# Attention: the queries of four tiles projected in one pass, and a new order of the work around them

## The chip, the cores and the metric

The kernel runs on one core of a Trainium2 chip. The metric is the device time of one execution in microseconds (us). The engines named below are TensorE (PE in the rows, with PEld for its weight loads), VectorE (DVE), ScalarE (ACT), GpSimd (POOL) and SyncE (SP). Each runs its own list of instructions strictly in program order and waits on semaphores for the others.

## The reference, cut to what matters

A token mixing product feeds a gated linear attention, and a two-layer local attention with feed-forward layers follows. The change is in the linear attention alone. The inputs are 4 batches of 1024 tokens of 256 features; there are 16 heads of 64.

```python
q, k, v = (split_heads(x @ W) for W in (Wq, Wk, Wv))       # x: layernorm of h
g = sigmoid(split_heads(x @ Wg + bg))
q = elu(q) + 1.0
k = elu(k) + 1.0
kv = einsum('bhnd,bhne->bhde', k, v)
k_sum = k.sum(axis=-2)
z = 1.0 / clip(einsum('bhnd,bhd->bhn', q, k_sum), 1e-06)
out = einsum('bhnd,bhde->bhne', q * SCALE, kv) * z[..., None] * g
h = h + merge_heads(out) @ Wo
h = h + ffn(layernorm(h))                                  # two layers, unchanged
```

## The kernel before

**Tiles and stages.** A tile is 128 tokens, so a batch has TB = 8 tiles. The 16 heads form PAIRS = 8 pairs of two. Each batch runs in two parts. The first loops over the 8 tiles: `keys` projects a tile, ScalarE takes the exponential, VectorE makes the feature elu + 1, and `g_products` adds the tile's share of x-transposed times k. Then `kv_products` makes kv. The second part runs over STAGES = 4 stages `u` of two tiles each. A stage projects its queries (`queries`), its gates (`gates`), multiplies queries by kv (`outputs`, in three groups of 5, 6 and 5 pairs over the two tiles, listed in `CUTS`), and lets VectorE divide and gate the result (`gated`). The following stage transposes that result (`out_transposes`), splits it in a high and a low part (`ot_hi` on ScalarE, `ot_lo` on VectorE), multiplies by Wo (`out_products`) and adds to the residual stream (`residual`). From stage 1 on, two tiles of the next batch are prepared beside it: `normalise`, `xt` (their transposes), `x_high` and `low`. In the last batch there is no next batch; VectorE and ScalarE prepare tables and weights of the local attention there (`scale_table`, the copies into `local_h` and the subtractions into `local_l`, and two `x_copy`).

**Precision by three products.** `matmul3` makes each product of three matmuls, from high and low parts of both operands (lines L117 to L119).

**Features of the queries.** `queries(b, u, f)` projects two pairs of heads for the two tiles of stage `u` into one PSUM bank: 12 matmuls of 256 columns. ScalarE's `exp_` (L512) reads the bank, and `feature` on VectorE does a min on the exponential (L648) and then adds the positive part out of the bank (L652) into the tile `qt` (attn_qT). Two banks, 0 and 1, take turns. A projection may start only when the feature made from the same bank's former filling is done:

```python
pe.wait_ge(*s.attn_feat.room(n, 2))
```

**Banks 6 and 7** take turns in the same way for all transposes and for the products with Wo: `room(k, 2)` on `attn_t_done` means that filling k waits until VectorE is done with filling k - 2. The order of the fillings of a stage is two halves of `out_transposes(…, 0)`, `out_products(…, 0)`, two halves of `out_transposes(…, 1)`, `out_products(…, 1)`, and then the two `xt` of the next batch, which VectorE frees in `low`.

**Outputs** use banks 4 and 5 without a second copy: `outputs` of a group waits until `gated` has read the group before (L700), and `gated` multiplies by the gate in L704. Stage `u` starts its first `outputs` only when all its features are there.

**What sets the order.** Nothing but the order in which the code of each engine is written; there is no scheduler. The functions below issue it.

## Time and profile before

| | |
|---|---|
| runs shown | 1814.84, 1820.49 and 1815.06 us, median 1815.06 us |
| profiled execution | 1819.65 us; span from first to last instruction 1817.9 us |
| mean granted clock of TensorE | 0.996 |
| busy time in the span | TensorE 1771.5 us, VectorE 1395.9 us, ScalarE 1003.8 us, GpSimd 528.0 us |
| attention's stages | the first matmul of the queries starts at 112.2 us, the last of the `outputs` at 605.5 us |

Times of rows are in microseconds from the start of the span. The busy time of TensorE counts overlapping matmuls once, and the start of the next matmul says more of its pace than the length of one: a matmul's own length holds the time through the array as well.

### The profile page before, as it was taken

The page shows a single profiled execution, that of the slowest core. Times are in us where ns is not written, and L with a number is a line of the kernel's source. Part 1 is how long each engine was busy: PE and PEld are TensorE (multiplying, and loading weights), DVE is VectorE, ACT ScalarE, POOL GpSimd, SP SyncE. Part 2 cuts the span into 40 slices and gives each one's busy share as a digit, 9 for nine tenths or more (in the row PEclk, how much of TensorE's full clock was granted, in tenths as well). Part 3 has the DMA queues.
Part 4 walks back from the last instruction along what each step waited for, and adds up shares of the span by engine and source line. Part 5 has one row for each costly group of instructions (what it writes and reads, how often), then busy time and mean ns, then how long its engine had stood idle before and what let it go on. Part 6 is the DMA issues. An engine that isn't in the chain of part 4 may idle for free. (4 is left out here: it accounts for less than half of the span.)

```text
span 1817.9 us, 52839 instructions
## 1 busy us (share of the span) xinstructions
PE 1771.5 (97%) x19744; PEld 1554.0 (85%) x19744; DVE 1395.9 (77%) x4325; ACT 1003.8 (55%) x2481; POOL 528.0 (29%) x382
## 2 busy tenths in 40 slices
PE   8999999999999989999999999999999999989998
PEld 7879889889888778888888888888888888888887
DVE  5877877877867788888888687767888888877774
ACT  4443443443434478888887444337777777743333
POOL 0000000000000256666666000016666666611111
PEclk9999999999999999999999999999999999999999
DMA  9200000000020111111111200002111111110011
GB/s 330 83 1 2 2 1 2 1 1 2 1 72 2 40 41 29 26 29 26 29 27 35 100 12 12 1 1 70 28 27 29 27 26 29 32 35 12 6 66 33
DMA packets 64830, 60.44 MB, mean 33 GB/s; under 512 B 16415, under 2 KB 59211, under 8 KB 64718
## 3 DMA queue, kind: packets, MB, share of 16 engines
q1 hardware_dynamic: 64718, 58.88, 10.9%
q8 instruction: 78, 1.28, 0.3%
q14 instruction: 34, 0.28, 0.1%
HBM read 33.95 MB, written 8.39 MB: 23 GB/s over the span
## 5 line engine op out<-in xcount | busy, mean ns | idle before, releaser
L1317 ACT ACTIVATE l_probs<-l_probs,l_negmax 128x192 f32<-128x192 f32 x512 | 225.8, 442 | 86.6 <-DVE l_negmax L1424 86.6
L1142 POOL TENSOR_TENSOR l_t<-l_t,l_rnorm 128x512 f32<-128x512 f32 x128 | 136.1, 1083 | 245.5 <-DVE l_rnorm L1096 245.5
L1264 POOL TENSOR_TENSOR l_probs<-l_probs,l_rowinv 128x768 f32<-128x768 f32 x128 | 185.1, 1466 | 20.1 <-DVE l_rowinv L1453 20.1
L117 PE MATMUL ps<-local_w_hi,l_xT 128*128 128x512 f32 x384 | 158.0, 412 | 1.6 <-PEq L1719 1.1
L1272 POOL TENSOR_TENSOR l_t<-l_t,l_t 128x1024 f32<-128x1024 f32 x62 | 146.9, 2370 | 30.0 <-DVE l_t L1110 18.4
L118 PE MATMUL ps<-local_w_lo,l_xT 128*128 128x512 f32 x384 | 151.6, 395 | 0.0
L119 PE MATMUL ps<-local_w_hi,l_xT 128*128 128x512 f32 x384 | 151.3, 394 | 0.0
L117 PE MATMUL ps<-m_hnT_hi,ffn_w_hi 128*128 128x512 f32 (+1 forms) x352 | 141.0, 400 | 0.0
L512 ACT ACTIVATE attn_exp<-ps 128x512 f32<-128x512 f32 x128 | 76.4, 599 | 116.1 <-PE ps L119 116.1
L119 PE MATMUL ps<-m_hnT_hi,ffn_w_lo 128*128 128x512 f32 (+1 forms) x352 | 138.5, 394 | 0.0
L118 PE MATMUL ps<-m_hnT_lo,ffn_w_hi 128*128 128x512 f32 (+1 forms) x352 | 138.4, 393 | 0.0
L488 POOL MEMSET l_xT<- 128x520 f32 x1 | 0.5, 532 | 463.9 <-PE ps L897 463.9
L1588 PE MATMUL ps<-l_probsT,l_v 128*64 128x64 f32 x2048 | 126.0, 225 | 1.7 <-DVE x L1392 1.0
L1588 PE MATMUL ps<-l_probsT,l_edge 128*64 128x64 f32 x2048 | 123.0, 222 | 0.0
L1105 DVE TENSOR_TENSOR l_t<-ps,rope_c 128x1024 f32<-128x1024 f32 x64 | 78.4, 1225 | 51.6 <-PE ps L1568 46.1
L1834 ACT ACTIVATE m_gelu<-ps,ffn_b 128x512 f32<-128x512 f32 x80 | 55.0, 687 | 110.4 <-PE ps L119 110.4
L1323 ACT ACTIVATE l_probsT<-ps 128x512 f32<-128x512 f32 x192 | 101.1, 598 | 18.9 <-PE ps L1575 14.2
L117 PE MATMUL ps<-attn_w_hi,attn_xT_hi 128*128 128x512 f32 x256 | 107.3, 419 | 3.5 <-issue 1.9
L1588 PEld LDWEIGHTS ps<-l_probsT,l_v 128*64 128x64 f32 x2048 | 104.2, 138 | 6.4 <-ACT l_probsT L1323 2.1
L525 ACT ACTIVATE attn_tanh<-ps 128x512 f32<-128x512 f32 x64 | 38.3, 598 | 121.1 <-PE ps L119 121.1
L1588 PEld LDWEIGHTS ps<-l_probsT,l_edge 128*64 128x64 f32 x2048 | 104.5, 138 | 0.0
L118 PE MATMUL ps<-attn_w_lo,attn_xT_hi 128*128 128x512 f32 x256 | 101.1, 395 | 0.0
(273 smaller groups left out, 5709.1 us busy)
## 6 DMA issues: line engine op xcount, KB each, us to landing
l_edge<-l_v SPq DMA_DIRECT2D x252, 64.0 KB, 2.0
tok_x<-x SPq DMA_DIRECT2D x16, 512.0 KB, 8.0
shifted<-x SPq DMA_DIRECT2D x64, 64.0 KB, 1.5
m_shifted<-shifted SPq DMA_DIRECT2D x16, 256.0 KB, 2.8
out<-x SPq DMA_DIRECT2D x8, 512.0 KB, 3.2
ffn_w_raw<-ffn_w SPq DMA_DIRECT2D x6, 640.0 KB
local_w_raw<-ffn_wqkv SPq DMA_DIRECT2D x4, 768.0 KB, 5.2
tok_base<-attn_base SPq DMA_DIRECT2D x4, 512.0 KB, 9.0
```

Of the source, the lines that this page charges most:

```text
L117: nc.tensor.matmul(out, wh, mh, start=start, stop=False, skip_group_check=True)
L118: nc.tensor.matmul(out, wh, ml, start=False, stop=False, skip_group_check=True)
L119: return nc.tensor.matmul(out, wl, mh, start=False, stop=stop, skip_group_check=True)
L512: nc.scalar.activation(ex[:, at % 2], ps[:, at % 2], ACT.Exp).then_inc(s.attn_exp.sem, 1)
L1105: nc.vector.tensor_tensor(t1[:].rearrange("p a (h d) -> p a h d", d=DH), q, cw, ALU.mult)
L1142: return nc.gpsimd.tensor_tensor(v, v, rn[:, a * LH:(a + 1) * LH].unsqueeze(2).to_broadcast([P, LH, DH]), ALU.mult)
L1264: nc.gpsimd.tensor_tensor(v, v, rinv[:, heads].unsqueeze(2).to_broadcast([P, LH // 2, REACH]), ALU.mult).then_inc(s.normal.sem, 1)
L1272: nc.gpsimd.tensor_tensor(t1[:], t1[:], t2[:], ALU.add).then_inc(s.summed.sem, 1)
L1317: last = nc.scalar.activation(v, v, ACT.Exp, bias=nb[:, h:h + 1], scale=-1.0, accum_out=rsum[:, h:h + 1])
L1323: nc.scalar.activation(pt[:, 4 * k:4 * k + 4].rearrange("p b q -> p (b q)"), ps[:, PT[k]], ACT.Copy).then_inc(s.p_done.sem, 1)
L1588: last = nc.tensor.matmul(ps[e * DH:(e + 1) * DH, OT, pair * P + tokens.start:pair * P + tokens.stop], keys, pt[:, 3 * pair + block, token ...
L1834: nc.scalar.activation(gl[:, c % 2], ps[:, bank + 1], ACT.Gelu, bias=K.b1[:, layer, HC + c:HC + c + 1]).then_inc(s.gelu.sem, 1)
```

## The change

Stages 0 and 1 now share their queries, and so do stages 2 and 3. `queries(b, u, *pairs)` projects one pair of heads for four tiles, so that one filling of a bank is 6 matmuls of 512 columns. There are 8 fillings for stages 0 and 1 (pairs 0 to 7) and 8 for stages 2 and 3, as many as before, of the same 512 columns. `query_features` does the min as before, and then writes the two halves of the bank apart: tiles of the even stage to `qt`, tiles of the odd stage to a new tile (`attn_qT_odd`), which lies where the parts of the keys lay. So the first of them in a batch waits for the last `g_products`. `outputs` of stages 0 and 1 wait for all 8 features.

The order around them is new on three engines:

- TensorE: the fillings of pairs 2 to 7 stand in one run behind `kv_products`. Stage 0 ends with the first `out_transposes` of stage 1 straight behind its last `outputs`, and one half of a gate later the product with Wo follows; the same at the end of stage 2. `out_transposes(…, 1)` stands straight behind `out_products(…, 0)` in stages 1 and 3. Pairs 0 and 1 of stage 2 are projected at the end of stage 1, and pairs 2 to 7 between the transposes and products of stage 2.
- VectorE: `take_kv` stands ahead of `variance` and of the subtraction for Wo's low part; three features stand behind those. At the end of stage 1 two features, with a gating between them, stand ahead of the next batch's `low`. In stage 2 the residual stands ahead of the second gating.
- ScalarE: the exponentials follow the queries' new order.

```diff
@@ -430,6 +430,8 @@
+    (qt_key,), _ = mem.place(mem.wb + 2 * INNER * 4, mem.wa, ("attn_qT_odd", [P, PAIRS, 2 * P], F32))
+    (qt_last,), _ = mem.place(mem.wa + KC * INNER * 4, mem.norm, ("attn_qT_odd_last", [P, PAIRS, 2 * P], F32))
...
+    def queries_of(b, u):
+
+        return qt if u % 2 == 0 else qt_last if b == B - 1 else qt_key
...
-            def query_feature(b, u, f):
-                feature(AB * b + 16 + 4 * u + f, f, qt[:, 2 * f:2 * f + 2, :])
+            def query_features(b, u, *pairs):
+
+                for m in pairs:
+                    n = AB * b + 16 + 4 * u + m
+                    dve.wait_ge(*s.attn_exp.after(n + 1))
+                    chain(nc.vector.tensor_scalar(ex[:, m % 2], ex[:, m % 2], 1.0, None, ALU.min))
+                    if u == 0 and m == 0:
+                        dve.wait_ge(*s.attn_g_mm.after(TB * b + TB))
+                    for w in range(2):
+                        cols = slice(2 * w * P, 2 * (w + 1) * P)
+                        done = nc.vector.scalar_tensor_tensor(queries_of(b, u + w)[:, m], ps[:, m % 2, cols], 0.0,
+                                                              ex[:, m % 2, cols], ALU.max, ALU.add)
+                    done.then_inc(s.attn_feat.sem, 1)
...
-                query_feature(b, 0, 0)
-                query_feature(b, 0, 1)
+                query_features(b, 0, 0, 1)
+                take_kv(b)
+                query_features(b, 0, 2, 3, 4)
                 early.variance(nc, chain) if last else norm.variance(nc, chain)
...
-                take_kv(b)
-                query_feature(b, 0, 2)
-                query_feature(b, 0, 3)
+                query_features(b, 0, 5, 6, 7)
...
+                    if u == 1:
+                        query_features(b, 2, 0)
+                        gated(b, 1, 2)
+                        query_features(b, 2, 1)
                     if not last:
                         for w in range(2):
                             low(b + 1, 2 * u - 2 + w)
...
-            def queries(b, u, f):
-                n = AB * b + 16 + 4 * u + f
-                pe.wait_ge(*s.attn_feat.room(n, 2))
-                for i in range(2):
-                    m = 2 * f + i
+            def queries(b, u, *pairs):
+
+                for m in pairs:
+                    n = AB * b + 16 + 4 * u + m
+                    pe.wait_ge(*s.attn_feat.room(n, 2))
                     for c in range(KC):
...
+                        tokens = slice(2 * u * P, (2 * u + 4) * P)
+                        last = matmul3(nc, ps[:, m % 2], wh[:, Q, c, m * P:(m + 1) * P], wl[:, Q, c, m * P:(m + 1) * P],
+                                       xth[:, c, tokens], xtl[:, c, tokens], c == 0, c == KC - 1)
+                    last.then_inc(s.attn_a_full.sem, 1)
...
-                queries(b, 0, 2)
-                queries(b, 0, 3)
+                queries(b, 0, 2, 3, 4, 5, 6, 7)
...
+                for u in range(STAGES):
+                    if u == 1 or u == 3:
+                        gates(b, 2 * u, (0,))
+                        if first and u == 1:
+                            pe.wait_ge(*s.attn_wo_lo.after(1))
+                        out_products(b, last, u, 0)
+                        out_transposes(b, last, u, 1)
+                        gates(b, 2 * u, (1,))
+                    if u == 2:
+                        queries(b, 2, 2)
+                        out_transposes(b, last, 2, 0)
+                        queries(b, 2, 3, 4)
+                        out_products(b, last, 2, 0)
+                        queries(b, 2, 5)
+                        out_transposes(b, last, 2, 1)
+                        queries(b, 2, 6, 7)
+                        gates(b, 4)
...
+                    if u == 1 or u == 3:
+                        out_products(b, last, u, 1)
+                    if u == 1:
+                        queries(b, 2, 0)
...
+                    if not ending:
+                        outputs(b, u, 2)
+                    if u == 0 or u == 2:
+                        out_transposes(b, last, u + 1, 0)
+                    if u == 1:
+                        queries(b, 2, 1)
+                    if not last and u % 2:
+                        for w in range(2):
+                            xt(b + 1, 2 * u - 2 + w)
```

How the order moves on VectorE is shown at two places. The first is batch 0, behind the features of the first fillings. L157 to L164 are `variance`, attn_wo_lo is the subtraction for Wo's low part, attn_kv the copy of kv, L648 and L652 (now L748 and L753) the two steps of a feature. Before:

```order
L163 TENSOR_SCALAR attn_rstd<-attn_rstd 128x8
L164 SCALAR_TENSOR_TENSOR attn_dev<-attn_tmp,attn_rstd 128x8
L764 TENSOR_TENSOR attn_wo_lo<-attn_wo_raw,attn_wo_hi 128x2048
L711 COPY attn_kv<-ps 128x260 x2
L648 TENSOR_SCALAR attn_exp<-attn_exp 128x512
L652 SCALAR_TENSOR_TENSOR attn_qT<-ps,attn_exp 128x512
```

Now, from the feature of pair 4 on:

```order
L748 TENSOR_SCALAR attn_exp<-attn_exp 128x512
L753 SCALAR_TENSOR_TENSOR attn_qT<-ps,attn_exp 128x256
L753 SCALAR_TENSOR_TENSOR attn_qT_odd<-ps,attn_exp 128x256
L157 TENSOR_REDUCE attn_rstd<-attn_stats 128x8
L158 TENSOR_SCALAR attn_mean<-attn_rstd 128x8
L159 TENSOR_TENSOR attn_dev<-attn_stats,attn_mean 128x16
L160 TENSOR_TENSOR attn_dev<-attn_dev 128x16
L161 TENSOR_REDUCE attn_tmp<-attn_dev 128x8
L162 TENSOR_REDUCE attn_rstd<-attn_stats 128x8
L163 TENSOR_SCALAR attn_rstd<-attn_rstd 128x8
L164 SCALAR_TENSOR_TENSOR attn_dev<-attn_tmp,attn_rstd 128x8
L792 TENSOR_TENSOR attn_wo_lo<-attn_wo_raw,attn_wo_hi 128x2048
```

The copy of kv moved ahead of both, and the statistics and the subtraction now stand between the features of pairs 4 and 5, in the middle of TensorE's run of projections.

The second place is the end of stage 1 on VectorE. L640 and L642 (now L656 and L658) are `low`, which frees banks 6 and 7; L678 (now L694) is `residual`; L714 to L720 are the four steps of a gating. Before:

```order
L678 TENSOR_TENSOR h<-ps,h 128x256
L640 TENSOR_TENSOR attn_xn_lo<-attn_xn,attn_xn_hi 128x256
L642 TENSOR_TENSOR attn_xT_lo<-ps,attn_xT_hi 128x2x128
L640 TENSOR_TENSOR attn_xn_lo<-attn_xn,attn_xn_hi 128x256
L642 TENSOR_TENSOR attn_xT_lo<-ps,attn_xT_hi 128x2x128
L648 TENSOR_SCALAR attn_exp<-attn_exp 128x512
```

Now:

```order
L694 TENSOR_TENSOR h<-ps,h 128x256
L748 TENSOR_SCALAR attn_exp<-attn_exp 128x512
L753 SCALAR_TENSOR_TENSOR attn_qT<-ps,attn_exp 128x256
L753 SCALAR_TENSOR_TENSOR attn_qT_odd<-ps,attn_exp 128x256
L714 TENSOR_SCALAR attn_den<-ps 128x10
L715 RECIPROCAL attn_z<-attn_den 128x10
L716 TENSOR_TENSOR attn_out<-ps,attn_z 128x640
L720 SCALAR_TENSOR_TENSOR attn_out<-attn_tanh,attn_out 128x640
L748 TENSOR_SCALAR attn_exp<-attn_exp 128x512
L753 SCALAR_TENSOR_TENSOR attn_qT<-ps,attn_exp 128x256
L753 SCALAR_TENSOR_TENSOR attn_qT_odd<-ps,attn_exp 128x256
L656 TENSOR_TENSOR attn_xn_lo<-attn_xn,attn_xn_hi 128x256
```

Ten instructions of features and gating moved in between the residual and `low`.

## Rows read from the trace of the kernel before

**Rows 1.** The page, busy time by engine (share of the span, instructions).

```profile
PE 1771.5 (97%) x19744; PEld 1554.0 (85%) x19744; DVE 1395.9 (77%) x4325; ACT 1003.8 (55%) x2481; POOL 528.0 (29%) x382
```

**Rows 2.** Timeline, TensorE, batch 1: start, length, line, tiles, [idle before <- releaser].

```profile
233.10 0.39 PE L117 MATMUL ps<-attn_k_hi,attn_xn_hi 128*128 128x512 f32 x1
...
251.23 0.39 PE L119 MATMUL ps<-attn_k_hi,attn_xn_lo 128*128 128x512 f32 x1
...
259.40 0.28 PE L118 MATMUL ps<-attn_xT_lo,attn_w_hi 128*128 128x256 f32 x1
...
262.03 0.28 PE L119 MATMUL ps<-attn_xT_hi,attn_w_lo 128*128 128x256 f32 x1
```

**Rows 3.** Timeline, ScalarE and VectorE, one filling's exponential and feature, batch 1.

```profile
262.35 0.60 ACT L512 ACTIVATE attn_exp<-ps 128x512 f32<-128x512 f32 x1 [0.84 <-PE ps L119]
...
296.52 0.60 ACT L512 ACTIVATE attn_exp<-ps 128x512 f32<-128x512 f32 x1 [0.84 <-PE ps L119]
...
297.15 0.43 DVE L648 TENSOR_SCALAR attn_exp<-attn_exp 128x512 f32<-128x512 f32 x1 [0.28 <-ACT attn_exp L512]
297.61 0.69 DVE L652 SCALAR_TENSOR_TENSOR attn_qT<-ps,attn_exp 128x512 f32<-128x512 f32 x1
```

**Rows 4.** Timeline, VectorE's feature in stage 1 and TensorE's projection behind it.

```profile
275.66 0.69 DVE L652 SCALAR_TENSOR_TENSOR attn_qT<-ps,attn_exp 128x512 f32<-128x512 f32 x1
...
276.41 0.39 PE L117 MATMUL ps<-attn_xT_hi,attn_w_hi 128*128 128x256 f32 x1 [0.32 <-DVE attn_qT L652]
```

**Rows 5.** Timeline, VectorE, batch 1: `low` of one tile and the residual.

```profile
292.31 0.42 DVE L678 TENSOR_TENSOR h<-ps,h 128x256 f32<-128x256 f32 x1 [2.01 <-PE ps L119]
293.84 0.43 DVE L640 TENSOR_TENSOR attn_xn_lo<-attn_xn,attn_xn_hi 128x256 fp32r<-128x256 f32 x1 [1.10 <-ACT attn_xT_hi L505]
294.18 0.42 DVE L642 TENSOR_TENSOR attn_xT_lo<-ps,attn_xT_hi 128x256 fp32r<-128x256 f32 x1
```

**Rows 6.** Timeline, VectorE, `variance` (first step, and what follows its eighth), batch 1.

```profile
259.50 0.17 DVE L157 TENSOR_REDUCE attn_rstd<-attn_stats 128x8 f32<-128x16 f32 x1
...
261.15 0.77 DVE L711 COPY attn_kv<-ps 128x260 f32<-128x260 f32 x2
```

**Rows 7.** Timeline, batch 0: the subtraction on VectorE and TensorE's wait for kv.

```profile
122.26 2.29 DVE L764 TENSOR_TENSOR attn_wo_lo<-attn_wo_raw,attn_wo_hi 128x2048 fp32r<-128x2048 f32 x1
...
125.33 0.47 PE L117 MATMUL ps<-attn_w_hi,attn_xT_hi 128*128 128x512 f32 x1 [1.90 <-issue]
```

**Rows 8.** Windows, batch 0: length, busy time by engine, granted clock (0.50), DMA.

```profile
126.40:129.50 3.10, 3.10 (x9) 2.31 (x7) 2.49 (x12) 0.60 (x1) 0.00 (x0) 0.50 0.00 0
```

**Rows 9.** Timeline, TensorE, batch 1: groups of `outputs`, and four transposes of `xt`.

```profile
264.99 0.81 PE L924 MATMUL ps<-attn_kv,attn_qT 64*64 64x65 f32 x40
265.73 0.50 PE L117 MATMUL ps<-attn_w_hi,attn_xT_hi 128*128 128x512 f32 x1
...
292.95 0.66 PE L855 MATMUL ps<-ident,attn_xn 128*128 128x128 f32 x4
293.36 0.36 PE L117 MATMUL ps<-attn_xT_hi,attn_w_hi 128*128 128x256 f32 x1
```

**Rows 10.** Timeline, VectorE, stage 1 of batch 1: a gating's first, third and fourth steps.

```profile
285.44 0.17 DVE L698 TENSOR_SCALAR attn_den<-ps 128x10 f32<-128x10 f32 x1 [0.56 <-PE ps L924]
...
285.89 0.82 DVE L700 TENSOR_TENSOR attn_out<-ps,attn_z 128x640 f32<-128x640 f32 x1
286.75 0.82 DVE L704 SCALAR_TENSOR_TENSOR attn_out<-attn_tanh,attn_out 128x640 f32<-128x640 f32 x1
```

**Rows 11.** Timeline, high parts on ScalarE and low parts on VectorE, two halves each.

```profile
297.01 1.08 ACT L534 ACTIVATE attn_oT_hi<-ps 128x512 fp32r<-128x512 f32 x2
...
298.21 1.28 DVE L671 TENSOR_TENSOR attn_oT_lo<-ps,attn_oT_hi 128x512 fp32r<-128x512 f32 x2
```

**Rows 12.** Timeline, last batch, end of stage 2 on ScalarE: weights, then `x_copy`.

```profile
583.16 2.00 ACT L597 ACTIVATE local_w_hi<-local_w_raw 128x1024 fp32r<-128x1024 f32 x2
585.05 1.08 ACT L546 ACTIVATE l_x<-h,l_shift,l_rstd 128x256 f32<-128x256 f32 x2
```

More of the change, by code:

```diff
@@ L806, in batch @@
                         x_lo(0)
+                    if u == 2:
+                        residual(b, last, u, 1)
                     gated(b, u, 1)
@@ L811, in batch @@
                         turn(0)
-                    residual(b, last, u, 1)
+                    if u != 2:
+                        residual(b, last, u, 1)
+                    if u == 1:
+                        query_features(b, 2, 0)
+                        gated(b, 1, 2)
+                        query_features(b, 2, 1)
                     if not last:
@@ L924, in outputs @@
                             last = nc.tensor.matmul(ps[tokens, 4 + e, at:at + OC],
-                                                    qt[r, m, which * P + half * DH:which * P + (half + 1) * DH], kv[r, m, :],
+                                                    queries_of(b, u)[r, m, which * P + half * DH:which * P + (half + 1) * DH], kv[r, m, :],
                                                     start=True, stop=True)
@@ L999, in batch @@
                 gates(b, 0)
-                outputs(b, 0, 0)
-                gates(b, 1, (0,))
-                outputs(b, 0, 1)
-                gates(b, 1, (1,))
-                queries(b, 1, 0)
-                outputs(b, 0, 2)
-                for u in range(1, STAGES):
-                    if u > 1:
-                        queries(b, u, 0)
-                    queries(b, u, 1)
-                    out_transposes(b, last, u, 0)
-                    queries(b, u, 2)
-                    queries(b, u, 3)
-                    if first and u == 1:
-                        pe.wait_ge(*s.attn_wo_lo.after(1))
-                    out_products(b, last, u, 0)
-                    gates(b, 2 * u, (0,))
-                    out_transposes(b, last, u, 1)
-                    gates(b, 2 * u, (1,))
-                    if last and u == STAGES - 1:
+                for u in range(STAGES):
[6 more added lines that the diff above has]
+                        gates(b, 2 * u, (1,))
+                    if u == 2:
+                        queries(b, 2, 2)
[6 more added lines that the diff above has]
+                        gates(b, 4)
+                    ending = last and u == STAGES - 1
+                    if ending:
                         x_t(0)
@@ L1024, in batch @@
                     gates(b, 2 * u + 1, (0,))
+                    if u == 2:
+                        out_products(b, last, 2, 1)
                     outputs(b, u, 1)
                     gates(b, 2 * u + 1, (1,))
-                    if last and u == STAGES - 1:
+                    if ending:
                         outputs(b, u, 2)
```

50 lines of the change are left out of this document (26 added, 24 removed).

## Prediction

> **What bounds the kernel now.** I read the page first: TensorE is busy 1771.5 of 1817.9 us, the next engine 1395.9 us [rows 1]. TensorE is full, so an edit pays only if it shortens TensorE's list or one of its waits, and costs as soon as it adds one. Then I read the timeline of batch 1, engine by engine, and looked at the starts of matmuls. In a full stretch 512 columns start every (251.23 - 233.10) / 80 = 0.2266 us, and 256 columns every (262.03 - 259.40) / 22 = 0.1195 us [rows 2]. Waits within the stages are few. The fourth projection of stage 1 in each batch waits for a feature: 0.32 us idle [rows 4] and 0.16 us more if one counts from its slot, since a matmul of 256 columns lasts 0.28 us and its slot is 0.12 [rows 2], so 0.48 us. In batch 0 TensorE waits 1.90 + 0.16 = 2.06 us for the copy of kv, held up behind Wo's subtraction [rows 7]. Half of the clock (0.50 of 2.4 GHz, so 1.2 GHz) was granted for about 3 us behind that wait [rows 8].
>
> **Fewer, wider matmuls.** A filling of a bank was 12 x 0.1195 = 1.434 us and is 6 x 0.2266 = 1.360 us [rows 2]. There are 16 fillings a batch before and after, 64 in all, with the same columns, so the sum is 64 x 0.0744 = **-4.8 us**. The Trainium skill says so from its side too: "TensorE: Matmul & The Clock Gate", section "Back-to-back issue gap", gives columns / 2.4 + 2.5 ns, by which the pieces are 109.2 and 215.8 ns and the whole gain would be 384 x 2.6 ns = 1.0 us. The rows disagree with it at both widths, and the sum goes by the rows.
>
> **Waits taken away.** The wait in stage 1, 0.48 us and 0.10 us for the slower first step behind a wait, goes with its projection: 4 x 0.58 = **-2.3 us** [rows 4]. In batch 0 the copy of kv comes earlier and 2.06 + 0.10 us go: **-2.2 us** [rows 7]. Whether the low clock goes too depends on the next waits; I leave it as it is (its 3.1 us at half speed cost 1.6 us [rows 8]).
>
> **The run of projections.** This decides. What must pass between the end of a filling and the next use of the same bank? The exponential starts 0.20 us behind the last matmul's slot (262.35 against 262.03 + 0.12) [rows 2, 3]. VectorE starts 0.63 us later, and its second step 0.46 us after that (296.52, 297.15, 297.61) [rows 3]. The second step was one instruction of 0.69 us. Now it is two of 256 columns. Rows of that width start 0.34 us apart and last 0.42 us [rows 5], which gives 0.76 us; it can't be under the 0.69 us of one of 512, nor above 2 x 0.69 = 1.38 us. I take 0.76, since those rows read PSUM at the same width. Then TensorE starts 0.06 us later (275.66 + 0.69, 276.41) [rows 4]. Sum: 0.20 + 0.63 + 0.46 + 0.76 + 0.06 = 2.11 us. The other bank's filling covers 1.36 us. So a run waits 0.75 us at every second filling. Before, no more than two projections stood in a row ahead of other work, so this never showed. Now six stand in a row (pairs 2 to 7), and pairs 4 and 6 wait: 2 x (0.75 + 0.10) = 1.7 us a batch.
>
> Pair 7 waits for more. Between the features of pairs 4 and 5 VectorE now does `variance`, 261.15 - 259.50 = 1.65 us [rows 6]. Stepped through for batch 1 from kv_products' end at 259.0: pair 4 projected 262.6 to 264.1, its feature done on VectorE at 266.0, `variance` to 267.65, feature 5 done and seen at 269.0; TensorE is through with pair 6 at 267.6. So 1.4 + 0.1 = 1.5 us more. In batch 0 Wo's subtraction (2.29 us, about 2.2 to the next start [rows 7]) is added: 3.7 us. In the last batch `variance` covers 24 tiles, 0.2 us more. Over four batches: 4 x 1.7 + 1.5 + 1.5 + 3.7 + 1.7 = **+15.2 us**.
>
> **Transposes behind outputs, stages 0 and 1.** The rsqrt steps now end later, so the first gating of stage 0 and both `outputs` behind it are some 0.5 us late. `out_transposes(1, 0)` has only half a gate (1.36 us) between itself and the product with Wo. The high part starts 0.2 us behind each half of the transposes, its second half ends about 1.1 us after its first start, and VectorE's low parts end 0.63 + 0.60 + 0.69 us after it [rows 11]; in all about 2.5 us from the transposes' start, against 0.8 + 1.36 that TensorE has: 0.4 + 0.1 us. The second half of `out_transposes(1, 1)` needs the residual (0.42 us, [rows 5], started 0.2 us after the product), with one half of the transposes (0.4) as its cover: 0.3 + 0.1 us. Sum 1.4 us, four batches: **+5.6 us**.
>
> **Features ahead of `low`, stage 2.** `out_transposes(2, 0)` takes bank 6, which `low` of the next batch frees. From the end of pair 0's projection VectorE needs 0.20 + 0.63 to its start, 1.14 for the feature (0.46 + 2 x 0.34), 2.06 for the gating (285.44 to 286.75, and 0.75 [rows 10]), 1.14 for the next feature and 0.34 + 0.42 + 0.06 for the first `low` [rows 5]: 5.99 us. TensorE has `outputs` (0.74, and 0.11 for the start behind it), a projection (1.36), `xt` (0.4) and another projection with its start (1.46) [rows 2, 9]: 4.07 us. It waits 1.9 us, and another 0.2 to 0.4 for bank 7. That is 2.3 us in batches 0 to 2, **+6.9 us**. What is late next is the transposes' product, but two projections cover it.
>
> **Stage 3.** `xt` now has only one group of `outputs` (0.85) ahead of `out_transposes(3, 0)`. `low` waits for the second gating (2.45 us from the end of `outputs(2, 1)`) and then needs 0.8 us; TensorE has half a gate, `xt` and `outputs`: 1.47 + 0.41 + 0.85, so 0.9 and then 0.4 us for the other bank. Another 0.3 and 0.4 us come as in stage 1. Together 2.0 us, batches 0 to 2: **+6.0 us**.
>
> **The last batch** has no `low`. But ScalarE makes weights and `x_copy` at the end of stage 2, 1.9 + 1.0 us in a row [rows 12], ahead of the high parts that the product of stage 3 now needs half a gate after its transposes: +2.3 us, with +0.4 as in stage 1. In stage 2 exponentials behind the same copies of stage 1, and VectorE's subtractions ahead of the feature of pair 5, cost about 1.0 and 1.4 us, and the second `outputs` of stage 1 0.4 us more than before. Sum **+5.5 us**.
>
> **Sum.** -4.8 - 2.3 - 2.2 + 15.2 + 5.6 + 6.9 + 6.0 + 5.5 = +29.9 us. The steps of the small latencies are rounded up here and there (0.05 us in some 40 waits), so I take +28 us. The profiled execution took 1819.65 us and would take 1847.7; it was 4.6 us above the median, and against 1815.06 the forecast is **1843 us**, 1.5% slower.
>
> **Rivals.**
> - *Only the wider matmuls and lost waits count* (8 in 100). It needs the bank's turn to take less than the 1.36 us of a filling; at the 2.11 us of the rows it can't. Then the time is 1815 - 4.8 - 2.3 - 2.2 - 1.6 = 1804 us. For it: each engine has slack on average (VectorE 77%, ScalarE 55% [rows 1]). Beside it stands the Trainium skill's "Perfetto Trace Analysis", section "Matmuls": larger matmuls are more efficient, and groups should rotate through banks so that one's evacuation overlaps the next's matmuls. The rotation through two banks is there; by the rows it is too short.
> - *The run of projections waits, the rest is absorbed* (14 in 100), because waits in the run delay TensorE and so let VectorE catch up before `low`: -9.3 + 15.2 = +6 us, 1821 us. Against it: `low` stands behind a feature that itself starts at a projection's end, so both are delayed alike.
> - *The clock falls more often* (18 in 100). Behind the wait of 2.1 us it fell to 1.2 GHz. Waits of 1.9 to 3.7 us now stand at one place in each of batches 0 to 2 and at one in the last, and each could cost the 1.6 us of [rows 8]: up to 4 x 1.6 more, 1850 us.
> - The forecast itself has 60 in 100, with 1832 to 1850 us as its own range.
>
> **How the numbers follow.** No change within 0.3% is 1810 to 1820 us, about what a measurement of this kernel can tell. Faster is the first rival, 0.08. Same takes the lower edge of the second, 0.05. Slower is the rest, 0.87. The range reaches from the second rival to above the third, 1819 to 1855 us; the unknown second step of the feature (0.69 to 1.38 us for both halves) is worth at most 0.6 us on some 8 to 12 waits and lies in it.
>
> **What the profile after would show.** TensorE's projections of the queries start 0.2266 us apart, and pairs 4, 6 and 7 of each batch wait 0.8, 0.8 and 1.4 us for attn_qT (pair 7 in batch 0: 3.6). `out_transposes` of stage 2 waits about 1.9 us for attn_xT_lo. TensorE's busy time falls by some 5 us while the span grows. VectorE's new step lasts about 0.42 us. What would make me wrong: a bank's turn under 1.5 us, or the transposes finding banks 6 and 7 free.

## The result, and the profile after

The changed kernel took 1847.73 us (median of 4 runs, 1847.51 to 1848.07) against 1816.12 us before on the same chip: ratio 1.0168, 95% interval 1.0156 to 1.018. It is 31.6 us slower. The forecast was 1843 us, the range 1819 to 1855. The profiled execution took 1847.88 us, its span is 1846.1 us (before 1817.9 us), the mean granted clock 0.996 in both. The 31.6 us rest on four executions of the kernel before, which spread from 1814.84 to 1820.49 us; timed 9 to 23 times beside the experiments it took 1817.0 to 1818.0 us, so the loss is nearer to 30 us. Between the two profiled spans it is 28.2 us.

The page, busy time by engine, answers to [rows 1]:

```profile
PE 1777.4 (96%) x19360; PEld 1530.3 (83%) x19360; DVE 1400.7 (76%) x4389; ACT 1006.3 (55%) x2481; POOL 528.0 (29%) x382
```

No engine's busy time grew by more than 5.9 us. So I cut the span at the starts of `kv_products` (batch 0, batch 3) and at the local layer's first product. Windows of the kernel before, three batches and the last one; the columns are length, busy time of PE, PEld, DVE, ACT, POOL (with counts), granted clock, DMA share, GB/s:

```profile
118.28:527.70 409.42, 406.39 (x3986) 357.05 (x3985) 305.09 (x653) 159.63 (x301) 0.00 (x0) 1.00 0.01 2
...
527.70:605.67 77.97, 76.70 (x1013) 68.29 (x1012) 60.92 (x125) 30.30 (x53) 0.53 (x1) 1.00 0.12 43
```

The same of the changed kernel:

```profile
117.09:547.41 430.32, 411.41 (x3698) 340.25 (x3697) 308.58 (x701) 161.92 (x301) 0.00 (x0) 0.99 0.01 1
...
547.41:635.44 88.03, 79.73 (x929) 64.49 (x929) 62.44 (x140) 30.71 (x53) 0.53 (x1) 0.98 0.10 38
```

The three batches lose 20.9 us and the last 10.1 us. The part ahead of the first cut is 1.2 us shorter (118.28 and 117.09), the part behind the local layer's first product 1.5 us; in each a low-clock stretch of the kernel before is absent (a stretch of 3.41 us in which TensorE was granted 1.2 in place of 2.4 GHz). In the three batches TensorE's idle time went from 3.0 to 18.9 us. The waits view of TensorE, changed kernel, same stretch (engine, tile, line and releaser: us in total, times, longest):

```profile
PE ps L117 <- DVE attn_qT_odd L753: 9.0, 9, 3.3
PE ps L971 <- DVE attn_xT_lo L658: 8.0, 6, 1.7
```

Before it had only these two:

```profile
PE ps L117 <- issue: 1.9, 1, 1.9
PE ps L117 <- DVE attn_qT L652: 0.9, 3, 0.3
```

So 17.0 of the 18.9 us are two waits, both for VectorE, both named in the prediction: the run of projections waits for features (three times a batch), and the transposes of stages 2 and 3 wait for `low` (twice a batch).

The run in batch 1. Timeline of TensorE, of pairs 2 to 7 the starts of those that waited:

```profile
268.43 0.39 PE L119 MATMUL ps<-attn_xT_hi,attn_w_lo 128*128 128x512 f32 x1
269.39 0.50 PE L117 MATMUL ps<-attn_xT_hi,attn_w_hi 128*128 128x512 f32 x1 [0.57 <-DVE attn_qT_odd L753]
269.73 0.40 PE L118 MATMUL ps<-attn_xT_lo,attn_w_hi 128*128 128x512 f32 x1
...
272.04 0.39 PE L119 MATMUL ps<-attn_xT_hi,attn_w_lo 128*128 128x512 f32 x1
272.99 0.50 PE L117 MATMUL ps<-attn_xT_hi,attn_w_hi 128*128 128x512 f32 x1 [0.56 <-DVE attn_qT_odd L753]
...
275.76 0.51 PE L117 MATMUL ps<-attn_xT_hi,attn_w_hi 128*128 128x512 f32 x1 [1.11 <-DVE attn_qT_odd L753]
```

Timeline of VectorE beside it, the features of pairs 4 and 5:

```profile
271.71 0.43 DVE L748 TENSOR_SCALAR attn_exp<-attn_exp 128x512 f32<-128x512 f32 x1 [1.01 <-ACT attn_exp L518]
272.18 0.42 DVE L753 SCALAR_TENSOR_TENSOR attn_qT<-ps,attn_exp 128x256 f32<-128x256 f32 x1
272.52 0.41 DVE L753 SCALAR_TENSOR_TENSOR attn_qT_odd<-ps,attn_exp 128x256 f32<-128x256 f32 x1
272.85 0.16 DVE L157 TENSOR_REDUCE attn_rstd<-attn_stats 128x8 f32<-128x16 f32 x1
...
274.49 0.43 DVE L748 TENSOR_SCALAR attn_exp<-attn_exp 128x512 f32<-128x512 f32 x1
274.95 0.42 DVE L753 SCALAR_TENSOR_TENSOR attn_qT<-ps,attn_exp 128x256 f32<-128x256 f32 x1
275.29 0.41 DVE L753 SCALAR_TENSOR_TENSOR attn_qT_odd<-ps,attn_exp 128x256 f32<-128x256 f32 x1
```

Read from above: pair 6 starts at 272.99, 0.47 us behind the start of the second step of pair 4's feature. Then VectorE does the statistics from 272.85 to 274.49, so pair 5's feature starts its last step only at 275.29, and pair 7 starts 0.47 us behind that. Where a wait stands, the start is later than the row's idle time says: 268.43 to 269.39 is 0.96 us where a slot is 0.23, so pair 4 started 0.73 us late and not 0.57. The next start follows 0.34 us behind (269.73), 0.11 us more than a slot, so the whole cost is 0.84 us. In batches 1 and 2 the three started 0.74, 0.73 and 1.28 us late, and each lost the 0.11 us besides: 3.1 us a batch.

Stage 2 of batch 1, timeline of VectorE from the feature of pair 0 to the last `low`:

```profile
304.19 0.43 DVE L748 TENSOR_SCALAR attn_exp<-attn_exp 128x512 f32<-128x512 f32 x1 [1.59 <-ACT attn_exp L518]
...
305.32 0.16 DVE L714 TENSOR_SCALAR attn_den<-ps 128x10 f32<-128x10 f32 x1
...
307.37 0.42 DVE L748 TENSOR_SCALAR attn_exp<-attn_exp 128x512 f32<-128x512 f32 x1
...
308.50 0.41 DVE L656 TENSOR_TENSOR attn_xn_lo<-attn_xn,attn_xn_hi 128x256 fp32r<-128x256 f32 x1
308.83 0.42 DVE L658 TENSOR_TENSOR attn_xT_lo<-ps,attn_xT_hi 128x256 fp32r<-128x256 f32 x1
```

And TensorE's transposes behind it:

```profile
307.29 0.40 PE L119 MATMUL ps<-attn_xT_hi,attn_w_lo 128*128 128x512 f32 x1
309.39 1.23 PE L971 MATMUL ps<-ident,attn_out 128*128 128x128 f32 x8 [1.71 <-DVE attn_xT_lo L658]
```

Feature, gating, feature, low, in a row without a gap: TensorE has nothing to do from 307.5 us until the first `low` is through. Its transposes start 1.88 us late, and their second half, which needs bank 7, loses 0.17 us more.

### The profile page after: what moved, and what is told of

Same layout as the page of the kernel before. It is cut to its first block and busy times, and to the rows that moved or that the text cites. A ratio compares the mean times of both kernels' runs of the same rounds, so it can differ in the third digit from the quotient of the medians.

```text
span 1846.1 us, 52139 instructions
## 1 busy us (share of the span) xinstructions
PE 1777.4 (96%) x19360; PEld 1530.3 (83%) x19360; DVE 1400.7 (76%) x4389; ACT 1006.3 (55%) x2481; POOL 528.0 (29%) x382
## 5 line engine op out<-in xcount | busy, mean ns | idle before, releaser
L119 PE MATMUL ps<-attn_w_hi,attn_xT_lo 128*128 128x512 f32 x256 | 100.9, 394 | 0.0
```

The costliest lines, as they stand in the source:

```text
L119: return nc.tensor.matmul(out, wl, mh, start=False, stop=stop, skip_group_check=True)
```

## The experiments

All changes below are against the changed kernel (e8 and e11: the kernel before). All eleven runs are timed in 5 rounds beside the kernel before, which took 1817.04 us (e1 to e4), 1817.94 us (e5 to e8) and 1817.97 us (e9 to e11). "Three batches" is the stretch between the `kv_products` of batches 0 and 3, 430.32 us in the changed kernel and 409.42 before. The diffs are cut to the lines that matter, and some are put in short form.

A gain below, as "-11.3 us", is against the 1847.73 us of the changed kernel, which was timed in the first round only, beside a kernel before of 1816.12 us. Counted from the kernel before of its own rounds, each would be 0.9 to 1.9 us better, so differences of 1 to 2 us between medians decide nothing. The lengths of single batches are surer. The table (all in us) has them from each run's trace, from one `kv_products` to the next, and for the last batch to the local layer's first product. Each * is 3.41 us at 1.2 GHz within that batch (** is one stretch of 6.83 us); batches 1 and 2 are free of them but for one.

| kernel | median | against the kernel before beside it | batch 0 | batch 1 | batch 2 | last |
|---|---|---|---|---|---|---|
| before | 1816.12 | | 138.88* | 135.27 | 135.27 | 77.98 |
| changed | 1847.73 | +31.6 | 146.69** | 141.79 | 141.83 | 88.03* |
| e1 | 1836.44 | +19.4 | 141.81 | 139.57 | 141.19* | 84.28 |
| e2 | 1839.25 | +22.2 | 140.68 | 140.37 | 140.47 | 86.07* |
| e3 | 1843.99 | +27.0 | 144.08* | 140.37 | 140.37 | 88.03* |
| e4 | 1849.13 | +32.1 | 145.97* | 142.43 | 142.47 | 88.34* |
| e5 | 1830.18 | +12.2 | 138.40 | 138.33 | 138.33 | 82.51 |
| e6 | 1840.05 | +22.1 | 143.42* | 139.75 | 139.77 | 86.33 |
| e7 | 1819.49 | +1.6 | 134.95 | 134.97 | 134.96 | 82.35 |
| e8 | 1816.89 | -1.1 | 138.75* | 135.10 | 135.10 | 77.30 |
| e9 | 1849.57 | +31.6 | 145.99* | 142.45 | 142.50 | 88.42* |
| e10 | 1815.26 | -2.7 | 134.94 | 134.97 | 135.12 | 77.97 |
| e11 | 1813.95 | -4.0 | 135.40 | 135.29 | 135.28 | 77.84 |

My theory was the prediction's: the loss is the sum of separate waits of TensorE, each for VectorE's list in its written order. The rivals: the cost is in the wider matmuls and the split feature themselves; or VectorE's load binds, and a wait that is taken away comes back elsewhere.

### e1: four banks for the run

```diff
-pe.wait_ge(*s.attn_feat.room(n, 2))
+pe.wait_ge(*s.attn_feat.room(n, 2 if u or m < 2 else 4))
-last = matmul3(nc, ps[:, m % 2], wh[:, Q, ...
+last = matmul3(nc, ps[:, bank(u, m)], wh[:, Q, ...
```

`bank(u, m)` is `(0, 1, 6, 7)[m % 4]` in stage 0 and `m % 2` elsewhere. The exponential and the feature read the same banks.

> The changed kernel took 1847.7 us. Here the six projections that stand in a row in stage 0 rotate through four PSUM banks (0, 1, 6, 7) in place of two; nothing else differs. Theory 1, the bank's turn as the prediction has it (2.11 us against 1.36 us of cover at pairs 4 and 6, and the statistics ahead of pair 5's feature at pair 7): those three waits go and nothing takes their place, 0.74 + 0.73 + 1.28 = 2.75 us in batches 1 and 2, 0.74 + 0.72 + 3.49 = 4.95 in batch 0, 0.74 + 0.75 + 1.52 = 3.0 in the last, so -13.5 us, 1834 us. Theory 2, VectorE's own work is the longer chain there (6 features at 1.14 us, the kv copy, variance, and the deviation steps behind them): TensorE gets ahead but then waits for the last feature and the first gating, some 0.5 us ahead of outputs(0, 0) and 0.9 us ahead of outputs(0, 1), so only about 2.2 us a batch come back, -8.6 us, 1839 us. Rival, the cost lies in the wider matmuls or in the feature's two halves and not in the waits: no change, 1847 to 1848 us.

Measured 1836.44 us, ratio 1.0103 (1.0088 to 1.0119), so -11.3 us. The three waits for features are gone from the run, and two stand at the `outputs` of stage 0. Timeline of TensorE, batch 1:

```profile
272.51 0.81 PE L962 MATMUL ps<-attn_kv,attn_qT 64*64 64x65 f32 x40 [0.17 <-DVE attn_qT_odd L757]
275.81 0.93 PE L962 MATMUL ps<-attn_kv,attn_qT 64*64 64x65 f32 x48 [0.89 <-DVE attn_out L720]
```

Batch 1 takes 139.57 us in place of 141.79. That is -2.2 us a batch, theory 2's number. The total lies between the two theories, because low clock went too: batch 0 gives 4.9 us, 2.7 more than batch 1, and the last 3.75 us, while one new stretch at 1.2 GHz came in batch 2. The short turn through two banks was real, but of the 3.1 us a batch that it and the statistics cost, 0.9 us only covered VectorE's longer chain.

### e2: statistics ahead of the first feature

```diff
+early.variance(nc, chain) if last else norm.variance(nc, chain)
+...                                   # Wo's subtraction, batch 0
 query_features(b, 0, 0, 1)
 take_kv(b)
 query_features(b, 0, 2, 3, 4)
-early.variance(nc, chain) if last else norm.variance(nc, chain)
-...
 query_features(b, 0, 5, 6, 7)
```

> The changed kernel with variance (and in batch 0 Wo's subtraction) ahead of the feature of pair 0, where VectorE waits for the exponential and for the last product of G, in place of between the features of pairs 4 and 5. Banks stay at two. If the wait ahead of pair 7 is that of the statistics, it falls from 1.28 to about 0 in batches 1 and 2, from 3.49 to 0 in batch 0 (and with it the half-clock stretch, 1.4 us), and by 1.5 in the last, while pairs 4 and 6 keep waiting 0.74 us each; part may come back at pair 7 as a bank's turn. Sum 1.4 + 1.4 + 3.6 + 1.7 = -8.2 us, and -1.4 if the clock stays up: 1838 to 1840 us. If pair 7 waits for something else, it stays where it is: 1847 us.

Measured 1839.25 us, ratio 1.0117 (1.0101 to 1.0132), -8.5 us. Waits of TensorE in the three batches:

```profile
PE ps L971 <- DVE attn_xT_lo L658: 8.0, 6, 1.7
PE ps L117 <- DVE attn_qT_odd L753: 3.5, 6, 0.6
```

From 9 waits for features six are left, of 0.6 us each: pairs 4 and 6. Pair 7's is gone, in batch 0 with the low clock at it: that batch gives 6.0 us, batch 1 only 1.4. The work was not made less, only moved to where VectorE stood idle.

### e3: `low` between two features

```diff
 query_features(b, 2, 0)
-gated(b, 1, 2)
+low(b + 1, 0)
+low(b + 1, 1)
 query_features(b, 2, 1)
...
 ot_lo(b, False, 2, 0)
+gated(b, 1, 2)
```

with `xt` ahead of `outputs(b, 1, 2)` on TensorE and `x_high` between the exponentials on ScalarE; batches 0 to 2.

> The changed kernel, stage 1 of batches 0 to 2: the next batch's transposes stand ahead of outputs(1, 2), its high parts between the exponentials of pairs 0 and 1, its low parts between the features of pairs 0 and 1, and gated(1, 2) behind the first low parts of stage 2. So out_transposes(2, 0) no longer stands behind a gating and a feature. Theory: its wait of 1.88 us and the 0.2 us of the second half go in three batches, -6.3 us; VectorE's gating then stands ahead of the features of pairs 3 and 4 and the last pair of stage 2 may wait 0.7 us for it, which would leave -4.4 us: 1841 to 1843 us. Rival, a wait that is taken away here comes back as the wait of stage 3 or in the keys of the next batch, since VectorE is busy all the time: 1846 to 1848 us.

Measured 1843.99 us, ratio 1.0148 (1.0133 to 1.0164), -3.7 us. Waits of TensorE in the three batches:

```profile
PE ps L117 <- DVE attn_qT_odd L757: 10.0, 12, 3.3
PE ps L979 <- DVE attn_xT_lo L662: 2.9, 3, 1.0
```

The waits for `low` fell from 8.0 to 2.9 us (those of stage 3 stay), and three new ones for features came, 1.0 us together, with their slower first steps: the gating of stage 1 now stands ahead of them. Batch 1 to batch 2 took 140.37 us, 1.42 less: the third of the expected 4.4 us that falls to a batch is 1.47. The median lies 1 us above the expected 1841 to 1843 us.

### e4 and e9: wide projections made of halves

```diff
-last = matmul3(nc, ps[:, m % 2], ..., xth[:, c, tokens], ...)
+for w in range(2):
+    last = matmul3(nc, ps[:, m % 2, 2 * w * P:2 * (w + 1) * P], ..., half w of the tokens, ...)
```

In e4 the loop over the halves is inside that over c, in e9 outside. e4's kernel leaves a part of the sums out, so it counts for its time alone.

> The changed kernel, each projection of 512 columns made as two of 256 columns (12 instead of 6 matmuls a pair), in the same order and with the same waits. It prices the wider matmuls alone. By the spacings 0.2266 and 0.1195 us a pair takes 0.0744 us more, 32 pairs 2.4 us, of which those that fill a bank another one waits for (some 8 to 12 of 32) are swallowed by shorter waits: +1.5 to +2.4 us, 1849.5 us. By the prediction's own term of 64 fillings it would be +4.8 us, 1852.5 us. If wide matmuls were what cost the time, it would fall toward 1816 us.

> As e4_halves (the changed kernel with each projection of 512 columns as two of 256, same waits), but with all six matmuls of the first 256 tokens ahead of the six of the second 256, as the kernel before had them inside its banks. e4_halves interleaved the two accumulations in one bank and so left a part of the sums out; its time was +1.4 us against the changed kernel. If the price of narrow matmuls is 0.0744 us a pair less what shorter waits swallow, this gives the same: +1 to +2.4 us, 1849 us. By the prediction's own 64 fillings: +4.8 us, 1852.5 us.

Measured 1849.13 us (e4) and 1849.57 us (e9; ratio 1.0168, 1.0155 to 1.0181), +1.4 and +1.8 us, but +32.1 and +31.6 us against the kernel before of their own rounds, where the changed kernel had +31.6. The medians show no difference beyond their noise, so the price has to come from the traces. The "32 pairs" of the first text were a slip: there are 16 fillings a batch, 64 in all, as the prediction had it. Windows, batch 1 to batch 2, of e9 (changed kernel 141.79):

```profile
264.39:406.84 142.45, 137.09 (x1330) 118.65 (x1329) 103.10 (x236) 54.11 (x101) 0.00 (x0) 1.00 0.01 1
```

Batch 2 gives 0.67, and e4 0.64 in both. So the wider matmuls gain 0.66 us a batch here, with 0.2 us more swallowed by shorter waits: 0.86 / 16 = 0.054 us a filling, where the prediction had 0.0744. The rows of the run above say why: (272.04 - 269.73) / 10 = 0.231 us between starts, not 0.2266. The wide matmuls are no rival for the loss.

### e5: both remedies of the run together

Edits of e1 and e2, and the rsqrt steps ahead of the first feature too.

> The changed kernel with four banks for the projections of stage 0 (as in e1_four_banks) and with variance, the rsqrt steps and Wo's subtraction ahead of the feature of pair 0 (more than in e2_variance_early: the rsqrt steps too). Alone, four banks gave -11.3 us and the early variance -8.5 us. If the three waits and the two that took their place at outputs(0, 0) and outputs(0, 1) are one chain (features at VectorE's pace with the statistics among them), then both together end it: of a batch's loss in the run only two waits of 0.1 to 0.2 us stay, -3.5 us in batches 1 and 2, -5.7 (and 1.4 of the clock) in batch 0, -4.1 in the last: -17 to -18 us, 1830 us. If the two overlap because they take away the same wait, the sum stays near the larger one: -11 to -12 us, 1836 us.

Measured 1830.18 us, ratio 1.0076 (1.0062 to 1.009), -17.6 us. In the three batches no wait for a feature is left:

```profile
PE ps L975 <- DVE attn_xT_lo L662: 8.1, 6, 1.7
PE ps L117 <- DVE attn_oT_lo L691: 0.6, 3, 0.3
```

More than half of the loss was the run. Alone the two gave 11.3 and 8.5 us, together 17.6. In batch 1, free of low clock in all of them, they gave 2.22 and 1.42 us alone, 3.46 together: the causes are mostly separate. The low clock of batch 0 is in both of the single gains and can go only once.

### e6: more cover in stages 1 and 3

```diff
-gates(b, 2 * u, (0,)); out_products(b, last, u, 0); out_transposes(b, last, u, 1); gates(b, 2 * u, (1,))
-outputs(b, u, 0); gates(b, 2 * u + 1, (0,))
+gates(b, 2 * u); out_products(b, last, u, 0)
+outputs(b, u, 0); gates(b, 2 * u + 1, (0,)); out_transposes(b, last, u, 1)
```

`ot_hi` and `ot_lo` of the moved transposes follow on ScalarE and VectorE; `out_transposes(3, 0)` and the next batch's `normalise` are moved as the text says.

> The changed kernel with its run of projections as it is, and these moves in stages 1 and 3: both halves of the gate ahead of the product with Wo, out_transposes(u, 1) behind outputs(u, 0) and half a gate, the next batch's normalised rows behind the low parts, and in batches 0 to 2 out_transposes(3, 0) behind the first half of gates(6). Theory, these waits come from too short a cover: T(1,0), the product of stage 1 and the second half of T(1,1) lose 0.3 + 0.35 + 0.26 us of their waits, stage 3 loses 1.17 + 0.19 + 0.25 but keeps 0.4 at the product, so about -2.75 us in each of batches 0 to 2 and -0.75 in the last: -9 us, 1838.7 us. Rival, out_transposes and low wait because VectorE has too much to do between the projections' run and there, wherever they stand: under -3 us, 1845 us or more.

Measured 1840.05 us, ratio 1.0125 (1.0109 to 1.014), -7.7 us. Waits of TensorE in the three batches:

```profile
PE ps L117 <- DVE attn_qT_odd L754: 9.0, 9, 3.3
PE ps L980 <- DVE attn_xT_lo L659: 5.1, 3, 1.7
```

Stage 3's wait for `low` is gone, stage 2's stays. Batch 1 gives 2.04 us where 2.75 were expected. Of the missing 0.7 us, 0.3 is a slip of the text: it promised T(1,0), the transposes `out_transposes(1, 0)`, its wait, but nothing had been moved there. The rest stays open. Against the kernel before of its own rounds the whole gain is 9.5 us, against the changed kernel's median 7.7; the medians don't say which.

### e7: all of them

> The moves of e5_banks_statistics, e3_low_early and e6_late_transposes together: the change's own wide projections and earlier kv copy stay, and its waits are taken away as far as an order allows. If the loss of 31 us is a sum of separate waits of TensorE, the gains add up: -17.5 - 4.4 - 9 = -31 us, and the clock falls seldomer: 1815 to 1818 us, level with the kernel before (1817.0 us), with about 0.8 us left ahead of the last pair of stage 2 and 0.4 us at the product of stage 3. If VectorE's load is what binds in a batch, the waits come back elsewhere: 1825 us or more.

Measured 1819.49 us (11 runs, 1816.67 to 1820.17), ratio 1.0005 (0.9995 to 1.0014): level with before, -28.2 us, and 1.5 us short of the 1815 to 1818 us expected. Windows, the three batches and the last:

```profile
117.75:522.64 404.89, 402.92 (x3697) 341.04 (x3697) 309.84 (x714) 159.37 (x301) 0.00 (x0) 1.00 0.01 2
...
522.64:604.99 82.35, 76.53 (x929) 63.68 (x928) 59.55 (x123) 30.30 (x53) 0.53 (x1) 1.00 0.11 40
```

The three batches are now 4.5 us shorter than before the change, the last still 4.4 us longer. Of the 4.5 us, 3.9 are batch 0, where the kernel before waits for kv and has its low clock; in batches 1 and 2 it is 0.3 us each. The gains of the parts (17.6, 3.7, 7.7) add to 29.0 us, and 28.2 came. Batch 1, which has no low clock in any of them, says it without the noise of medians: 3.46 + 1.42 + 2.04 = 6.92 us, and 6.82 came. This leaves little room for the rival that VectorE's load binds and a wait taken away comes back elsewhere.

### e10: the last batch as before

> e7_all_waits in batches 0 to 2, and in the last batch the kernel before's own order with narrow projections (queries for two tiles at once in every stage). In e7_all_waits the stretch from kv_products of the last batch to the local layer's first product took 82.35 us, in the kernel before 77.97 us; batches 1 and 2 took 134.97 us against 135.27. Theory: the rest of the loss sits in the last batch alone, so -4.4 us against e7_all_waits: its profiled span of 1814.9 becomes 1810.5 us, the median 1815 us, 2 to 4 us under the kernel before. Rival, the last batch's order hardly matters since the local layer waits for something else: no change against e7_all_waits, 1819.5 us.

Measured 1815.26 us (12 runs), ratio 0.9979 (0.9971 to 0.9988), 2.7 us under the kernel before. The last batch takes 77.97 us in place of 82.35: the gain came from there, as expected. Windows, the three batches:

```profile
117.56:522.59 405.03, 403.07 (x3710) 341.76 (x3709) 306.76 (x695) 159.44 (x301) 0.00 (x0) 1.00 0.01 2
```

### e8 and e11: the kernel before, with the kv copy earlier

```diff
+early.variance(nc, chain) if last else norm.variance(nc, chain)
+...                                   # Wo's subtraction; in e8 the rsqrt steps too
 query_feature(b, 0, 0)
 query_feature(b, 0, 1)
-early.variance(nc, chain) if last else norm.variance(nc, chain)
-...
 take_kv(b)
```

> The kernel before, narrow projections in its own order; only VectorE's order in stage 0 differs: the kv copy directly behind the feature of the second group, and variance, the rsqrt steps and Wo's subtraction ahead of the first feature, where VectorE waits for TensorE. It is the one part of the change that takes a wait away, done alone. Theory: in batch 0 the wait of 2.0 us for the kv copy goes, with the low clock behind it (1.6 us), and 0.3 us at outputs(0, 1) in each batch: -3.4 to -5 us against the kernel before, 1812 to 1814 us. If that wait was in the shadow of something else: no change, 1817 us.

Measured 1816.89 us, ratio 0.9994 (0.9985 to 1.0003): no difference, where I had expected 3.4 to 5 us. Batch 0, VectorE:

```profile
116.62 2.29 DVE L762 TENSOR_TENSOR attn_wo_lo<-attn_wo_raw,attn_wo_hi 128x2048 fp32r<-128x2048 f32 x1
118.83 0.16 DVE L130 TENSOR_SCALAR attn_rstd<-attn_dev 128x8 int32<-128x8 int32 x1
...
120.83 0.43 DVE L648 TENSOR_SCALAR attn_exp<-attn_exp 128x512 f32<-128x512 f32 x1
121.29 0.69 DVE L652 SCALAR_TENSOR_TENSOR attn_qT<-ps,attn_exp 128x512 f32<-128x512 f32 x1
```

and TensorE:

```profile
118.28 1.69 PE L897 MATMUL ps<-attn_wv,attn_out 128*64 128x65 f32 x52
122.04 0.38 PE L117 MATMUL ps<-attn_xT_hi,attn_w_hi 128*128 128x256 f32 x1 [2.07 <-DVE attn_qT L652]
```

The wait for kv was exchanged for one for the first feature: with the 2.0 us of rsqrt steps behind Wo's subtraction, that feature was late. e11 leaves these steps where they were.

> As e8_before_plus (the kernel before with the kv copy directly behind the second feature), but with only variance and Wo's subtraction ahead of the first feature; the rsqrt steps stay where the kernel before has them. In e8_before_plus batch 0 kept a wait of 2.27 us, now ahead of the projections of group 2, because 2.0 us of rsqrt steps and 2.2 us of subtraction both stood ahead of the first feature. In e2_variance_early the same two steps left 0.34 us there. Theory: the 2.06 us of batch 0 fall to 0.3 to 0.4 us and the clock stays at 2.4 GHz there: -1.7 and -1.6 us, 1814 to 1815 us. Rival, the low clock comes anyway somewhere else: -1.7 us or less, 1816 to 1817 us.

Measured 1813.95 us (11 runs), ratio 0.9976 (0.9967 to 0.9985), 4.0 us under the kernel before: the fastest kernel here. The first feature's start moves from 120.83 to 118.85, and TensorE goes on at 120.06. Batch 0 is 3.5 us shorter than before, and batches 1 and 2 are as they were: the gain is the one wait and the low clock that had followed it. Windows, the three batches:

```profile
117.91:523.88 405.97, 404.69 (x3986) 356.00 (x3985) 305.44 (x655) 159.66 (x301) 0.00 (x0) 1.00 0.01 2
```

e10, with wide projections in its first three batches, needs 405.03 us for them, e11 405.97. The 0.9 us between them isn't the price of wide projections alone: the two orders differ, and both kernels still have waits (TensorE is idle for 2.0 us of that stretch in e10 and for 1.3 us in e11). Together, wide projections and their order bring 0.3 us a batch over e11.

## Why the prediction was right, point by point

- **The mechanism held.** Every wait that it named stood at its place, and the run of projections was the largest. The bank's turn of 2.11 us against a cover of 1.36 us gave 0.75 us and, with 0.10 for the slower first step, 0.85 us each for pairs 4 and 6; measured were 0.74 and 0.11. By batch its terms add up to 7.2, 7.1, 7.1 and 8.5 us; measured were 7.8, 6.5, 6.6 and 10.1 us, the first and the last with low clock in them that the terms had left out. The stretches ahead of and behind attention were 2.8 us shorter, which makes 28.2.
- **The step that was off by 4.7 us** is none of the kernel's. For the profiled execution the forecast was 1847.7 us, and it took 1847.88. From that the prediction took off the 4.6 us by which the kernel before's profiled execution lay above the median of the runs shown. The changed kernel's four executions lie within 0.6 us of each other, so there was nothing to take off. That the profiled time came out to 0.2 us is partly luck, since the terms miss in both directions (below) and 1.9 us were taken off the sum as rounding, which no row showed.
- **Pair 7:** predicted 1.5, 1.5, 3.7 and 1.7 us with the slower first step; measured 1.39, 1.39, 3.6 and 1.63 with it. The run as a whole: +15.2 predicted, 13.5 us as late starts and 14.8 with the twelve slower first steps. e5 gave back 17.6 us. In batch 1 it gave 3.46 us, 3.1 of them the run's and 0.34 the wait of `outputs` for the late first gating of stage 0; in batch 0 and the last one low clock went too.
- **Fewer, wider matmuls:** -4.8 us was mis-sized. By e9 it is 0.86 us a batch, -3.4 us, of which 0.66 a batch show. The prediction took the pace of the keys' products (0.2266 us) for that of the queries (0.231 us). The sentence on the Trainium skill there ("TensorE: Matmul & The Clock Gate", "Back-to-back issue gap") uses a formula that the Trainium skill gives for a single matmul in isolation, and not for a stream of weight loads and matmuls as here. The 1.0 us worked out from it is not borne out; the measured 3.4 lies between it and the forecast.
- **Waits taken away:** the kv wait and those of stage 1 are gone; -2.2 and -2.3 us is their price in the kernel before. In batch 0 of e11, where the first went alone, 3.5 us came, 1.6 of them the low clock that the prediction had left standing. e8 shows that the first was not free for the taking: what else stands ahead of the copy decides.
- **Transposes behind outputs:** 1.4 us a batch predicted. Measured 0.34 (`outputs`, [0.18] in the row below), 0.29, 0.35 and 0.26 us, 1.24 together. Timeline of TensorE, batch 1:

```profile
282.64 0.93 PE L958 MATMUL ps<-attn_kv,attn_qT 64*64 64x65 f32 x48 [0.18 <-DVE attn_out L716]
...
288.77 0.39 PE L117 MATMUL ps<-attn_wo_hi,attn_oT_hi 128*128 128x256 f32 x1 [0.18 <-DVE attn_oT_lo L687]
```

- **Features ahead of `low`:** 1.9 us and 0.2 to 0.4 behind it; measured 1.88 and 0.17 us. But e3, which took it away, gave 1.42 us a batch back and not 2.1. VectorE's gating had to stand somewhere.
- **Stage 3:** 2.0 us predicted, 1.8 measured: transposes 1.17 us in place of 0.9, the other bank 0.17 in place of 0.4, product 0.19 and second half 0.25 in place of 0.3 and 0.4. The 0.9 doesn't follow from the terms beside it, which give 2.45 + 0.8 - 1.47 - 0.41 - 0.85 = 0.5 us. That this term came near is luck.
- **The last batch:** its stretch grew by 10.06 us. The terms had 3.4 us for the run, 1.4 for the transposes and 5.5 for the rest, less 1.8 for the wide matmuls and the wait of stage 1: 8.5 us. The high parts behind the weights and `x_copy` made the product of stage 3 wait 2.1 us, forecast at 2.7, and what the terms lack is the low clock behind that wait, about 1.6 us. The terms of 1.0, 1.4 and 0.4 us were not tested one by one. Timeline of TensorE:

```profile
621.50 0.39 PE L117 MATMUL ps<-attn_wo_hi,attn_oT_hi 128*128 128x256 f32 x1 [1.92 <-DVE attn_oT_lo L687]
```

- **Rivals.** *Only the wider matmuls count* fell with the result. *The rest is absorbed* fell with e6 and e3, whose gains came out of just these waits. *The clock falls more often* was half true: within attention the changed kernel's profile has one stretch of 3.41 us more in batch 0 and one more in the last batch, about 3 us of time, and elsewhere two fewer, about as much. The granted clock was low for 17.7 us in both profiled executions.
- **A sign that I had wrong:** TensorE's busy time should have fallen by 5 us and rose by 5.9 (1771.5 to 1777.4). In the three batches, 5.0 of it. At each wait the profile counts 0.27 us of what is lost as busy (0.84 us lost at pair 4, 0.57 idle), and low clock adds busy time too. e7 shows it: with the same matmuls and almost no waits, TensorE is busy for 402.92 us in the three batches, 8.5 us less than the changed kernel and 3.5 less than the kernel before. With waits in play the busy time of TensorE is no measure of its work.

The Trainium skill's rule that one group's evacuation should overlap the next one's matmuls through rotating banks ("Perfetto Trace Analysis", "Matmuls") is what e1 tests. It agrees: four banks in place of two gave 11.3 us. By the turn (2.11 us) against the fill (1.36 us), three banks should do, since two fillings cover 2.72 us; this was not tried.

What stays open: how the clock shares in the medians. Between the two profiled spans, which differ by 28.2 us, it makes up next to nothing. The medians differ by 31.6 us, as the profiled execution of the kernel before was 3.5 us above its median; low clock would account for that (in the later rounds its executions under 1816 us had a mean clock of 0.997 to 0.999, those over 1819 us 0.994 to 0.997), but no record has the clock of these executions one by one.

## What to carry to other kernels

Before work of one kind is put in a row, compare the time from a bank's last matmul until it is free again with the time that the other banks' fillings cover. Each place where the first is longer costs the difference and a slower first matmul (0.11 us here), and more banks or other work between them is the cure. Statistics and other side work of VectorE belong where it stands idle (here ahead of the first feature, worth 8.5 us in e2 and 4.0 us in e11, low clock included), but count what fits: 2 us too many, and the wait only moves (e8). When separate waits add up in a batch, each can be priced from one timeline and tested alone; the sum of the parts here was 6.92 us in a batch, and together they gave 6.82.

## What the runs showed of the hardware

A low clock goes with some long waits and not with others. Windows of the changed kernel, at the end of the wait of 3.3 us (batch 0) and behind that of 1.92 us (last batch); the clock column reads 0.56 and 0.57, and at half the clock (1.2 of 2.4 GHz) it stood for most of each, 6.83 us from 130.6, while TensorE still waited, and 3.41 us from 622.1:

```profile
131.20:138.20 7.00, 6.92 (x18) 5.38 (x18) 3.88 (x17) 1.19 (x2) 0.00 (x0) 0.56 0.00 0
622.00:626.00 4.00, 4.00 (x24) 4.00 (x23) 1.46 (x2) 0.00 (x0) 0.00 (x0) 0.57 0.01 2
```

In e5 TensorE waited 1.93 us at the same product of the last batch, and in e1 2.36 us in batch 0, and the clock behind both stayed full:

```profile
602.70:606.70 4.00, 3.89 (x31) 3.65 (x32) 2.72 (x6) 0.37 (x1) 0.00 (x0) 1.00 0.01 2
...
132.80:138.00 5.20, 4.23 (x98) 3.37 (x99) 4.41 (x18) 0.60 (x1) 0.00 (x0) 1.00 0.01 3
```

What such a stretch costs: e1 had one of 3.41 us in batch 2, behind the 1.71 us wait of stage 2 that left the clock full in the other batches. It took 141.19 us for that batch, 1.6 us more than for batch 1 with the same waits:

```profile
398.71:539.90 141.19, 136.96 (x1233) 114.19 (x1233) 100.19 (x228) 53.98 (x101) 0.00 (x0) 0.99 0.01 2
```

Matmuls of 512 columns do not always start 0.2266 us apart: those of the queries in the run took 0.231 us, at full clock.
